# GNN layer and 64-expert FFN on one core: neighbour sums taken by rows, shared pieces, base addition and gathers moved in the expert loop

## What is computed

```python
# graph layer, on h = _layernorm(x)
agg = jax.ops.segment_sum(h[src], dst, num_segments=N)   # 10625 edges, sorted by dst
t = (1.0 + eps) * h + agg
t = relu(batch_norm(t @ W1 + b1, g1, be1))               # 512 -> 1024
x = x + h + relu(batch_norm(t @ W2 + b2, g2, be2))       # 1024 -> 512
# mixture of experts, on y = _layernorm(x)
shared = sum(_swiglu_ffn(y, sWg[e], sWu[e], sWd[e]) for e in range(2))
top_w, top_i = jax.lax.top_k(softmax(y @ Wr), 6)         # 64 experts, weights of 512x512
routed = sum(_swiglu_ffn(y, Wg[e], Wu[e], Wd[e]) * gate[:, e:e+1] for e in range(64))
out = x + shared + routed + y
```

## Time and profile before

| | us |
|---|---|
| median of 3 runs | 772.82 (771.66 to 773.99) |
| the profiled execution, its own time | 773.9 |
| its span | 772.2 |
| start of the product with W1 | 63.7 |
| gate of expert 1 starts | 181.8 |
| last down product ends | 758.3 |
| TensorE busy | 714.7 (93%) |

### The profile page before, as it was taken

One profiled execution on the slowest core, in us unless ns is written; L12 is line 12 of the kernel. 1 busy time (PEld: TensorE's weight loads), 2 busy tenths in 40 slices (PEclk: granted clock), 3 DMA queues, 4 the chain that ended last, 5 costly groups with the idle time before them and its releaser, 6 DMA issues. The chain is left out here.

```text
span 772.2 us, 17458 instructions
## 1 busy us (share of the span) xinstructions
PE 714.7 (93%) x7096; PEld 485.1 (63%) x7096; DVE 260.2 (34%) x788; ACT 196.8 (25%) x497; POOL 171.7 (22%) x157
## 2 busy tenths in 40 slices
PE   2599999879999999999999999999999996999991
PEld 2597777556776666555566666655557774777760
DVE  7982624976112442222212212122332221222110
ACT  1222422311332222221122222212112331333331
POOL 4000000011222222232232213222333312222222
PEclk9999999999999999999999999999999998999997
DMA  8970020434999999999999999999999999999951
GB/s 259 407 296 3 0 109 21 169 113 158 371 359 349 350 379 392 395 385 391 373 390 386 380 388 384 393 384 386 382 388 380 374 358 344 373 371 371 371 137 24
DMA packets 57264, 236.34 MB, mean 306 GB/s; under 512 B 6171, under 2 KB 6335, under 8 KB 40286
## 3 DMA queue, kind: packets, MB, share of 16 engines
q1 hardware_dynamic: 46004, 211.33, 71.4%
q0 software_dynamic: 10144, 20.56, 11.4%
q10 hardware_dynamic: 1034, 3.30, 1.1%
HBM read 222.32 MB, written 12.83 MB: 305 GB/s over the span
## 5 line engine op out<-in xcount | busy, mean ns | idle before, releaser
L1362 PE MATMUL ps<-ring,xT 128*64 128x256 f32 x1296 | 153.6, 382 | 0.0
L424 POOL DMA_INDIRECT xg<-x_tab,idx_sb x64 | 68.9, 1076 | 368.0 <-DVE idx_sb L937 201.9
L436 POOL DMA_INDIRECT out<-ysb,idx_sb x64 | 92.5, 1445 | 217.5 <-issue 180.2
L1362 PEld LDWEIGHTS ps<-ring,xT 128*64 128x64 f32 x1296 | 91.1, 137 | 44.3 <-issue 1.6
L930 DVE TENSOR_REDUCE gates<-ps 128x1 f32<-128x3 f32 (+1 forms) x62 | 10.0, 162 | 285.8 <-PE ps L1270 277.4
L623 ACT ACTIVATE ysb<-ps 64x256 f32<-64x256 f32 x64 | 24.2, 378 | 260.6 <-PE ps L1362 211.3
L1362 PE MATMUL ps<-ring,hTj 128*64 128x256 f32 x624 | 76.3, 387 | 0.0
L1362 PE MATMUL ps<-w,xT 128*64 128x256 f32 x608 | 71.9, 381 | 0.0
L898 DVE TENSOR_TENSOR onehot<-iotaAB,slotv 125x640 bf16<-125x640 f32 (+1 forms) x64 | 67.3, 1051 | 1.4 <-PE ps L1278 1.0
L1362 PEld LDWEIGHTS ps<-ring,hTj 128*64 128x64 f32 x624 | 42.5, 138 | 30.5 <-issue 12.6
L1362 PEld LDWEIGHTS ps<-w,xT 128*64 128x64 f32 x608 | 42.5, 137 | 20.4
(11 more groups left out here) (237 smaller groups left out, 820.9 us busy)
## 6 DMA issues: line engine op xcount, KB each, us to landing
ring<-in_L_ffn_Wg SPq DMA_DIRECT2D x41, 1024.0 KB
ring<-in_L_ffn_Wu SPq DMA_DIRECT2D x40, 1024.0 KB
ring<-in_L_ffn_Wd SPq DMA_DIRECT2D x39, 1024.0 KB
w<-in_L_ffn_Wd SPq DMA_DIRECT2D x20, 1024.0 KB
w<-in_L_ffn_Wg SPq DMA_DIRECT2D x19, 1024.0 KB
w<-in_L_ffn_Wu SPq DMA_DIRECT2D x19, 1024.0 KB
ring_x<-in_L_ffn_Wu SPq DMA_DIRECT2D x5, 1024.0 KB
ring_x<-in_L_ffn_Wd SPq DMA_DIRECT2D x5, 1024.0 KB
```

The costliest lines, as they stand in the source:

```text
L424: g.indirect_dma_start(out=xg[j % NX][0:ROWS[j], :], out_offset=None, in_=x_tab, in_offset=bass.IndirectOffsetOnAxis(ap=idx_sb[0:ROWS[j], ...
L436: g.indirect_dma_start(out=out, out_offset=bass.IndirectOffsetOnAxis(ap=idx_sb[0:ROWS[j], j:j + 1].bitcast(u32), axis=0), in_=ysb[j % NY][ ...
L1362: last = t_.matmul(ps[h * BIG:(h + 1) * BIG, bank, 0:AW], big(k), w[:, k, h * AW:(h + 1) * AW], start=(k == 0), stop=(k == KD - 1))
```

## The change

- The neighbour sums are taken by rows: `aggregate` has the count block as the stationary operand and h0's 512-wide rows as the moving one, in two parts `h0_hi` (h0 rounded to float32r, written by ScalarE) and `h0_lo` (the rest, one VectorE subtraction per tile). That is 10 float32r matmuls of 125x512 per block in place of 20 float32 ones of 125x125. The result (rows, not columns) is joined with (1+eps) h0 on VectorE (`h_rows`), and 4 transposes on TensorE bring it to columns; `at_diag` is gone. Block b is aggregated right behind its visits.
- `one_m` is compared from two int16 tiles: `iota_m` is spread over the group, and ScalarE spreads the columns ahead (`spread`, 25 copies of 125x625). `one_s` stays.
- Ring slots 4 to 7 hold h0_hi, h0_lo and the spread columns at first, so SyncE issues their loads when hT is ready.
- In small steps the up product stands right behind the gate product.
- The shared pieces go to steps 6 to 34, the base behind scatter(36), and from step 43 a gather is issued one scatter earlier.

```diff
-    BASE_AFTER = 47
+    BASE_AFTER = 36
-        free = [j for j in range(FIXED, FIXED + E - LAST - NBIG) if j not in (SPREAD + 4, SPREAD + 5)]
+        free = [j for j in range(FIXED, 35) if j not in (SPREAD + 4, SPREAD + 5)]
@@ sync
+                if i == 4:
+                    sp.wait_ge(s_hT, T)
@@ gpsimd
             for j in range(E + LAG):
-                if j < E:
+                if j < E and j <= BASE_AFTER + LAG + 1:
                     gather(j)
                 if j >= LAG:
+                    if BASE_AFTER + LAG + 1 < j + 1 < E:
+                        gather(j + 1)
                     scatter(j - LAG)
                 if j == BASE_AFTER + LAG:
                     add_base()
@@ scalar
+            def spread(b):
+                for g in range(b * GB, (b + 1) * GB):
+                    if g >= NREP:
+                        act.wait_ge(s_sm, g - NREP + 1)
+                    sc.activation(rep[g % NREP][:], col_m[:, g * U:(g + 1) * U].unsqueeze(2).broadcast_to([P, U, P]),
+                                  ACT.Copy).then_inc(s_rep, 1)
@@ vector
+                if spread:
+                    last = v.tensor_tensor(one_m[slot][:], iota_m[:], rep[g % NREP][:], ALU.is_equal)
-            def at_diag(b):
-                dve.wait_ge(s_atc, 2 * b + 2)
-                sl = aT[b % 2][:, b, :]
-                v.scalar_tensor_tensor(sl, ident[0:P, 0:P], eps1[:], sl, ALU.mult, ALU.add).then_inc(s_at, 1)
+            def h_rows(b):
+                dve.wait_ge(s_agg, b + 1)
+                if b >= 2:
+                    dve.wait_ge(s_hrT, b - 1)
+                v.scalar_tensor_tensor(hrow[b % 2][:], h0[:, b, :], eps1[:], ps[0:P, 4 + b % 2, :], ALU.mult,
+                                       ALU.add).then_inc(s_hrow, 1)
+            for t in range(T):
+                v.tensor_tensor(h0_lo[:, t, :], h0[:, t, :], h0_hi[:, t, :].bitcast(f32), ALU.subtract).then_inc(s_lo, 1)
@@ tensor
-            def aggregate(from_aT, bank):
-                for d in range(KD):
-                    for s in range(T):
-                        last = t_.matmul(ps[:, bank, d * P:(d + 1) * P], h0[:, s, d * 128:(d + 1) * 128],
-                                         from_aT[:, s, :], start=(s == 0), stop=(s == T - 1))
+            def aggregate(from_aT, bank, done):
+                for s in range(T):
+                    for part in (h0_hi, h0_lo):
+                        last = t_.matmul(ps[0:P, bank, :], from_aT[:, s, :], part[:, s, :],
+                                         start=(s == 0 and part is h0_hi), stop=(s == T - 1 and part is h0_lo))
@@
-                both = j >= 1 and CAPS[j] > BIG
+                both = j >= 1
```

More of the change, by code:

```diff
@@ L164, in gnn_moe_kernel @@
         ring_x = rH0.place("ring_x", [128, KD, 512], f32)
-        aT = [rAT.place(f"aT{i}", [P, T, P], f32) for i in range(2)]
+        aT = [rAT.place(f"aT{i}", [P, T, P], f32r) for i in range(2)]
+        iota_m = rAT.place("iota_m", [P, U, P], i16)
+        hrow = [rAT.place(f"hrow{i}", [P, D], f32) for i in range(2)]
+        rep = [rAT.place("rep0", [P, U, P], i16)]
         rAT.rewind()
@@ L208, in gnn_moe_kernel @@
         cntS = rWin.place("cntS", [128, E], f32)
-        ring = [rOh.place(f"ring{i}", [128, KD, 512], f32) for i in range(8)]
+        ring = [rOh.place(f"ring{i}", [128, KD, 512], f32) for i in range(4)]
+        upper = rOh.at
+        ring += [rOh.place(f"ring{4 + i}", [128, KD, 512], f32) for i in range(4)]
+        past = rOh.at
+        rOh.at = upper
+        h0_hi = rOh.place("h0_hi", [P, T, D], f32r)
+        h0_lo = rOh.place("h0_lo", [P, T, D], f32r)
+        rep += [rOh.place(f"rep{i}", [P, U, P], i16) for i in range(1, NREP)]
+        assert rOh.at <= past
+        rOh.at = past
         w2 = [rOh.place(f"w2_{i}", [128, KD, 512], f32) for i in range(2)]
@@ L695, in columns, with group_onehots @@
                 return v.tensor_tensor(col_m[:], ps[0:P, 6, 256:256 + NV], grp_of[:], ALU.subtract)
-            def group_onehots(g, slot):
+            def group_onehots(g, slot, spread):
                 c = slice(g * U, (g + 1) * U)
-                for one, iota, col in ((one_s, iota_s, col_s), (one_m, iota_m, col_m)):
-                    last = v.tensor_tensor(one[slot][:], iota[:].unsqueeze(1).broadcast_to([P, U, P]),
-                                           col[:, c].unsqueeze(2).broadcast_to([P, U, P]), ALU.is_equal)
+                v.tensor_tensor(one_s[slot][:], iota_s[:].unsqueeze(1).broadcast_to([P, U, P]),
+                                col_s[:, c].unsqueeze(2).broadcast_to([P, U, P]), ALU.is_equal)
+                if spread:
+                    last = v.tensor_tensor(one_m[slot][:], iota_m[:], rep[g % NREP][:], ALU.is_equal)
+                else:
+                    last = v.tensor_tensor(one_m[slot][:], iota_m[:], col_m[:, c].unsqueeze(2).broadcast_to([P, U, P]),
+                                           ALU.is_equal)
                 last.then_inc(s_sm, 1)
@@ L1108, in visits, with row_transposes, block_transposes @@
                     visit(g, g % NSM, 2 * (b % 2))
[L1110 to L1115 removed]
+            def aggregate(from_aT, bank, done):
[3 more added lines that the diff above has]
+                                         start=(s == 0 and part is h0_hi), stop=(s == T - 1 and part is h0_lo))
+                last.then_inc(done, 1)
             def block_aggregate(b):
[L1118 removed]
+                pe.wait_ge(s_atc, 2 * b + 2)
                 if b == 0:
[L1120 removed]
+                    pe.wait_ge(s_lo, T)
+                if b >= 2:
+                    pe.wait_ge(s_hrow, b - 1)
+                aggregate(aT[b % 2], 4 + b % 2, s_agg)
+            def row_transposes(rows, bank, done):
+                for k in range(KD):
+                    last = t_.transpose(ps[:, bank, k * P:(k + 1) * P], rows[:, k * 128:(k + 1) * 128], ident[0:P, 0:P])
+                last.then_inc(done, 1)
+            def block_transposes(b):
+                pe.wait_ge(s_hrow, b + 1)
                 if b >= 2:
                     pe.wait_ge(s_hT, b - 1)
[L1123 removed]
+                row_transposes(hrow[b % 2], 6 + b % 2, s_hrT)
             pe.wait_ge(s_code, 2)
```

131 lines of the change are left out of this document (86 added, 45 removed).

## The result

The changed kernel takes 792.65 us in the median of 4 runs (791.5 to 793.14), the kernel before 773.34 in the same series: a ratio of 1.0245, 95% interval 1.0224 to 1.0265. It is slower by 19.3 us. The forecast was 787. The profiled execution is one of 792.5, with a span of 790.8.

A forecast was written before the change was run, and what follows sets the result against it. TensorE was taken to pace, with weight DMA and the scatter chain close behind. -7.2 + 28.0 + 2.9 - 8.5 = +15.2 on 773.9 gave 789, 788 against the median, less 1: 787 us; range 768 to 798.

The forecast's parts named there:

- A: Rival, late steps: the chain of scatters does not bind, as scatters of unloaded steps land sooner; total 770; chance 0.15.
- B: Rival, late steps: the gather is not held by the base; stage 75.6 to 80 us, total 759; chance 0.10.
- C: Rival, neighbour sums: float32r goes like float32, 9.3 us a block; W1 at some 87, total 818; chance 0.05.
- D: Rival, neighbour sums: the one-hot comparison gains nothing and stays at 0.72 us; W1 at 62.5, total 793; chance 0.12.
- Ahead of the experts: Neighbour sums before the expert loop: faster one_m and float32r aggregates start W1 at 56.5 instead of 63.7, -7.2 us.
- The slow first aggregate: Ahead of W1: first aggregate at half pace, 7.00 against 4.68; a slow clock into W1 may give back 1 to 3 us.
- Gate and up adjacent. The same instructions: Small expert steps: reordering the up product costs at most 0.1 us a step, taken as nothing.
- S35: Start of step 35, claimed to come 28.0 us later because seven shared pieces move into steps 6 to 34.
- The late steps: Steps 35 to 46: 75.6 us of TensorE, 20.8 stall, 10 at scatter pace; 106.4 against 103.5, +2.9 us.
- the episode: From the scatter ahead of the base to TensorE's use of the gather behind it: 29.5 us, carried over from before.
- The chain can be a little faster: Late steps: scatters may beat 8.33 us while the weight queue is shorter; 1 us taken off, 788 to 787.
- Large steps: Steps after the small ones: the 6.55 us hole and about 2 of slow clock behind it go, -8.5 us.

The follow-up runs named there:

- e2: Kernel before with only the shared pieces moved to steps 6 to 34: 793.23 us, ratio 1.0251.
- e6: Kernel after with odd experts' rows scattered to a second table never joined with the output, each scatter waiting for the one two ahead: 767.74 us.
- e7: Kernel after without the addition of the base, so shared result and x are missing from the output: 781.46 us.
- e4: Kernel after with gathers 42 and 43 issued ahead of the base: 789.51 us.
- e8: e1 with the up product right behind the gate product in small steps as well: 769.1 us, ratio 0.9918 to the kernel before.
- e1: Kernel after with the expert loop of before, so only the new stretch ahead of the experts: 768.55 us, ratio 0.992 to the kernel before.
- e3: Kernel after with only the base put back behind scatter 47: 788.99 us.
- e12: Kernel after with weights of experts 35 to 50 loaded only by half, the rest of the slot keeping old values: 769.04 us.
- e9: e1 with 14 products that nobody reads, in TensorE's gaps ahead of W1: 766.82 us, ratio 0.9903 to the kernel before.
- e5: Kernel after with a fourth ysb buffer for the experts' results: 789.2 us.
- e10: e8 with e9's products and odd experts up to 39 in a second table, read back in SyncE's queue and added ahead of the base: 777.71 us.
- e11: e10 with the second table's read issued by ScalarE in step 44 instead of SyncE's queue: 773.1 us.

## Why the prediction was near, and where its steps failed

**The mechanism** was the forecast's: a stall for a gather in step 41 with a slow clock behind it, steps 42 to 46 at the pace of scatters, no hole in the large steps. It came so. e2 shows that the pieces alone cost 18.6 us, e6 that the waits for scatters make the loss, e7 that the base alone does not. Rivals A, B, C and D fall: the spacing was 8.68, not TensorE's 6.30 (A); gather 42 was used at 567.56, 0.7 us after the base let scatter 37 go (B); float32r goes at 0.23 for 512 columns (C); one_m went to 0.39 (D). Nor would B's 759 have come with the gathers in front, as e4 shows: the prediction saw only the gather behind the base, and in truth the copy of expert 40's result stands behind it too. Rival C's own sum is off by a little, without effect: 31, 46.5, 4.8 and 3 give 85, not 87.

**Ahead of the experts**: W1 at 56.31 for 56.5 said, one_m 0.39 (midway between the 0.42 taken and the 0.36 also worked out), float32r 0.23 for 0.26, the last one-hot starts at 48.9, for an end of 49.8 said. The term was -7.2 and is -5.9, the difference being W1's first products at 1.2 GHz, which was named as 1 to 3 us but not put into the sum. ScalarE's spreads took 0.62 each for 0.85 said. The slow first aggregate (7.00 for 4.68), which the prediction took for a sign of a slow clock, is none by the profile: the granted clock reads 1.00 from 27 to 40 in the kernel before. The new kernel has the same, its first float32r products stand 0.43 apart (30.73 to 32.87) and later ones 0.23, at a reading of 1.00; why is not shown.

**"Gate and up adjacent. The same instructions"**, taken as nothing: the step that failed. The pieces did move S35 by the 28.0 (e2: 27.7), but a step with a piece is 0.24 us shorter in the new order, 23 times, and S35 came 22.4 later. The traces of the kernel after and of e8 show it in such steps; what in the sequence saves it was not tried. In e8, where the pieces stay spread and scatters are the limit, this gain does not reach the end.

**The late steps** were mis-sized: +9.7 for +2.9. Steps 42 to 46 took 41.3 us, 8.25 each in the mean for 8.3 said, though unevenly (6.3 to 10.6). The stall is the rest: 25.86 for 20.8, of which 2.1 is the chain (scatter 36 at S35 + 35.4 for 33.3; 8.68 a scatter for 8.33) and 3.1 the episode (32.6 for 29.5), and some 2 us of slow clock in step 41 that had no term. "The chain can be a little faster", the 1 us taken off, had the wrong sign.

**Large steps**: -7.7 for -8.5.

The errors on both sides, -5.6 in the early steps and +6.8 in the late ones, nearly cancel. That is luck, and 787 for 792.65 looks better than its terms. Of the parts tried alone, the pieces cost 18.6 us (e2) and the stretch ahead of the experts gains 6.1 (e1). That makes 12.4 of the measured 19.3; some 3.7 of the rest are the base's new place (e3), and some 3 stay open.

## What to carry to other kernels

Where two chains run at nearly the same rate, moving work from one stretch to another is worth only the slack of the other chain: count it in each stretch (here 8.6 us a step against 8.3 to 8.7 a scatter, so none) before taking work out. A stall that has several things queued behind it changes its name when one of them is moved; look for all that wait for the same landing. An improvement that a profile shows step by step can be gone at the end, so follow it to the next joint wait, here the base.

## What the runs showed of the hardware

- A scatter with accumulation, each waiting for the one ahead, goes every 8.3 to 9.5 us (means over a stretch: 8.33 in the kernel before, 8.68 in the kernel after, 9.5 in e8) beside weights at 370 to 395 GB/s, every 7.6 at 267 (e12), and every 4.7 once the weights are in (the last ones of e9, 739.04 to 748.50).
- A step with a shared piece takes 0.24 us less when gate and up stand together (10.62 for 10.86 and 9.84 for 10.08, e8 and e1), though its instructions are the same.
- The granted clock fell in some profiled executions of one and the same code and not in others. It was below 1.00 ahead of W1, from 51 on, in e1, e3, e6 and e8; only at the start of W1 in the kernel after and e7; and 1.00 up to 160 in e4, e5 and e12. Between 160 and 176 it fell again in all of these but e5, and in the kernel before (0.72 from 170 to 176).
- A read of 1.25 MB in rows of 2 KB, put between weights in their queue, held SyncE for 13.36 us (e10); the three weight items of 1 MB just ahead of it took 1.6 to 3.0 there, a later one 9.26. The same read issued by ScalarE held that engine for 1.1 (e11).
